# Owners and the square root placed earlier on ScalarE, keep from the minimum itself, one copy of the turned keys

## The chip, the cores and the metric

One Trainium2 chip, one core of it. The metric is the device time of one launch in microseconds (us). A NeuronCore has five engines with instruction streams of their own: PE (TensorE, matmuls and transposes), VectorE (DVE), ScalarE (ACT), GpSimd (POOL) and SyncE (SP), which in this kernel only issues transfers. They meet in semaphores.

## The reference

```python
N, HEADS, HEAD_DIM = 4096, 8, 32            # x: (4096, 256) f32, adj: (4096, 4096) int32 of 0 and 1
Q, K, V = (x @ W.T).reshape(n, HEADS, HEAD_DIM).transpose(1, 0, 2)   # for WQ, WK, WV
energy = Q @ we.T + be
attn = jnp.einsum('hqd,hkd->hqk', Q, K) * SCALING + energy
attn = softmax(attn + jnp.where(adj > 0, 0.0, -jnp.inf), axis=-1)
hard = (attn == jnp.max(attn, axis=-1, keepdims=True)).astype(jnp.float32) / HEADS
out = jnp.einsum('hqk,hkd->hqd', hard, V).transpose(1, 0, 2).reshape(n, EMBED)
return layernorm(x + out)                    # eps 1e-5
```

Each query takes, per head, the value of its one best neighbour. The adjacency is sparse and uneven: low-numbered nodes have many neighbours, later ones few.

## The kernel before, in words

A prologue (about 185 us) computes Q, keys and values for all nodes; keys (scaled by a negative factor, so that the best is a minimum) and values, split into three bf16 parts, go to a table in DRAM. The main loop then walks over *items*. A tile is 128 queries, a group is 32 queries of it (GQ), and an item is one group with up to 372 (3 x 124) of the nodes that any of its queries has as neighbour. There are 200 items. A turn of the loop holds four items, b = 0..3 (RING), and all engines run the same turns with their own code. For an item m the steps are:

- ScalarE `owners` (L624): from the edges of the group's lists, which list slot belongs to which node (`reached`, bf16); PE `planes_of` (L1207) multiplies it with the tile's words (`pay`) into `ps_x`.
- VectorE `pick` (L928 to L943): from the planes the node numbers and adjacency words (`hit`, `hit_vals`, `picks`, `bits`).
- GpSimd `gather` (L532): three indirect transfers fetch keys and values of the picked nodes into `kv`; `queries` (L525) copies the group's queries.
- ScalarE `masks` (L656) spreads the adjacency bits to bf16.
- PE `keys_across` (L1245) transposes the keys into `ps_both`, ScalarE `keys` (L662) copies them to `k_t`, PE `scores` (L1222, L1227) multiplies with the queries and adds the mask, into the same banks of `ps_both` (two buffers, one for even and one for odd items, each of two banks, one for each half of the heads).
- VectorE `tops` (L951 to L958): `best`, the minimum of each row and half; `minus_top`, the running minimum over the items of a group (`cap_of` cuts it off at a group's first item), and `keep`, 1 where the running one stays.
- ScalarE `hards` (L667): the marks, the sign of minimum minus score; PE `hards_across` (L1237) turns them into `ps_h`, ScalarE `hard_rows` (L652) copies them to `hard_t`, PE `values` (L1257) multiplies them with the values into `ps_o`.
- VectorE `merge` (L968): `o_all = o_all * keep + ps_o`.

These are staggered. In its body b of a turn PE runs planes of item b+4, scores of b+1, values of b-1, marks of b and key transposes of b+2, in that order. ScalarE runs masks of b+2, the marks' copy of b, owners of b+5, keys of b+2 (two halves, each with its own semaphore), then `hards` of b+1. VectorE runs pick of b+4, tops of b+1, merge of b-1. PE's values of an item wait for the merge of the item before (one `ps_o`).

Three other kinds of work are put between, each under a branch with a flag that SyncE plans. The *front end* turns a tile of adjacency (128 x 4096 int32) into words: ScalarE casts four quarters (`cast`, L605, `joined`), quarter 0 behind `hards` of b = 0, quarters 1 and 2 around `hards` of b = 1, quarter 3 in b = 2; PE multiplies each (L1162, `words`) one body later. The *finish* (L871 to L908 on VectorE, L1167 to L1187 on PE, L610 on ScalarE) makes the words' ranks and lists. The *rows* of a finished tile: VectorE transposes `o_all` to `o_t` in b = 1 (L974), PE turns it (`rows_back`, L1267), VectorE in b = 2 adds x and takes mean and variance (L981 to L988), ScalarE takes the square root (`row_std`, L673), and VectorE takes its reciprocal and scales the row (`norm_rows`, L992 and L995), which SyncE stores. In b = 2 ScalarE's quarter 3 stands ahead of the square root, and VectorE's `norm_rows` ahead of the merge.

## Time and profile before

| | us |
|---|---|
| three runs | 1316.35 median, 1309.31 to 1316.83 |
| the profiled execution | 1317.37, of which its span is 1315.6 |
| busy in the span: PE, weight loads | 951.6 (72%), 616.6 |
| VectorE, ScalarE, GpSimd | 929.0 (71%), 892.0 (68%), 632.8 |
| first and last start of the marks' copy (L652, 200 of them) | 185.1 and 1279.1 |
| HBM | 221 GB/s over the span |

The profile is one execution as the hardware profiler took it. Its parts: busy time per engine, the span in slices, the chain of work that ended last, the costliest groups of instructions; and the trace behind it can be asked for windows (busy time in stretches), waits (who waited for whom) and the timeline. In a timeline row the two numbers are start and duration, then engine, line, operation, out<-in with shapes, and in brackets the idle time of the engine ahead of it and what ended that. Consecutive instructions of one kind are merged (x2). "Issue" is idle time in which the engine waited for nothing that the profile shows: its own register and branch work. Granted clock is the share of full speed that TensorE was given.

### The profile page before, as it was taken

The page shows a single profiled execution, that of the slowest core. Times are in us where ns is not written, and L with a number is a line of the kernel's source. Part 1 is how long each engine was busy: PE and PEld are TensorE (multiplying, and loading weights), DVE is VectorE, ACT ScalarE, POOL GpSimd, SP SyncE. Part 2 cuts the span into 40 slices and gives each one's busy share as a digit, 9 for nine tenths or more (in the row PEclk, how much of TensorE's full clock was granted, in tenths as well). Part 3 has the DMA queues.
Part 4 walks back from the last instruction along what each step waited for, and adds up shares of the span by engine and source line. Part 5 has one row for each costly group of instructions (what it writes and reads, how often), then busy time and mean ns, then how long its engine had stood idle before and what let it go on. Part 6 is the DMA issues. An engine that isn't in the chain of part 4 may idle for free.

```text
span 1315.6 us, 51593 instructions
## 1 busy us (share of the span) xinstructions
PE 951.6 (72%) x14758; PEld 616.6 (47%) x14759; DVE 929.0 (71%) x2616; ACT 892.0 (68%) x1688; POOL 632.8 (48%) x820
## 2 busy tenths in 40 slices
PE   4787648777777778777787777777777777777771
PEld 2343325454544555455454545455445545455540
DVE  5444536777878777777787777777777777778880
ACT  1523347778777787777877877877777777766770
POOL 0000065675656566555565555554554455445650
PEclk9988877999999998989999899989998989989995
DMA  4634468677687787678777878778878787756770
GB/s 155 214 128 160 145 201 279 196 231 255 197 263 217 243 253 234 215 242 266 248 207 231 268 226 262 252 230 272 257 235 258 248 251 254 254 180 194 212 213 4
DMA packets 89522, 291.06 MB, mean 221 GB/s; under 512 B 16984, under 2 KB 30040, under 8 KB 89496
## 3 DMA queue, kind: packets, MB, share of 16 engines
q0 software_dynamic: 48720, 199.60, 49.5%
q1 hardware_dynamic: 40776, 91.15, 20.4%
q8 instruction: 12, 0.20, 0.1%
q14 instruction: 14, 0.11, 0.0%
HBM read 275.98 MB, written 14.71 MB: 221 GB/s over the span
## 4 chain that ended last, share of the span: by engine, by line
DVE 26%; PE 25%; issue 20%; ACT 15%; DVEq 7%; DMA 3%; ACTq 2%; SPq 1%; POOL 1%; POOLq 0%
DVE best L951 6%; ACT joined L605 5%; PE ps_both L1222 4%; ACT k_t L662 4%; PE ps_both L1154 4%; DVE picks L941 3%; PE ps_h L1237 3%; PE ps_o L1257 3%; DVE hit_vals L934 3%; PE ps_r L1267 3%; DVE hit L928 2%; PE ps_both L1227 2%; ACT hard L667 2%; PE ps_both L1144 2%; DVE o_all L968 2%
## 5 line engine op out<-in xcount | busy, mean ns | idle before, releaser
L532 POOL DMA_INDIRECT kv<-kv_table,picks x309 | 294.9, 954 | 231.3 <-DVE picks L941 127.6
L532 POOL DMA_INDIRECT early<-kv_table,picks x300 | 286.2, 954 | 246.0 <-DVE picks L941 131.6
L652 ACT ACTIVATE hard_t<-ps_h 128x768 bf16<-128x768 bf16 x200 | 162.0, 810 | 233.1 <-PE ps_h L1237 227.4
L667 ACT ACTIVATE hard<-ps_both,minus_top 128x384 bf16<-128x384 f32 x402 | 214.1, 594 | 32.9 <-DVE minus_top L955 30.3
L1222 PE MATMUL ps_both<-k_t,q_now 32*32 32x384 f32 x3216 | 192.6, 534 | 32.1 <-ACT k_t L662 29.0
L951 DVE TENSOR_REDUCE best<-ps_both 128x2 f32<-128x768 f32 x201 | 190.7, 949 | 28.0 <-PE ps_both L1227 17.8
L1207 PE MATMUL ps_x<-pay,reached 128*128 x1224 | 120.2, 233 | 99.6 <-ACT reached L624 93.3
L662 ACT COPY k_t<-ps_both 128x384 f32<-128x384 f32 x404 | 171.6, 479 | 14.4 <-PE ps_both L1245 14.3
L968 DVE SCALAR_TENSOR_TENSOR o_all<-o_all,keep,ps_o 128x96 f32 x400 | 107.7, 311 | 61.8 <-issue 26.5
L1207 PEld LDWEIGHTS ps_x<-pay,reached 128*128 128x128 bf16 x1224 | 83.7, 102 | 137.5 <-ACT reached L624 128.0
L605 ACT ACTIVATE joined<-adj_in,minus_half 128x1024 bf16<-128x1024 int32 x128 | 147.9, 1164 | 0.0
L1227 PEld LDWEIGHTS ps_both<-mask_of,masked 128*128 128x128 bf16 x1206 | 72.9, 102 | 140.9 <-issue 140.9
L525 POOL COPY q_now<-q_t 128x64 f32 x202 | 50.4, 249 | 167.4 <-issue 164.3
L656 ACT ACTIVATE masked<-bits,one 124x384 bf16<-124x384 uint32 x202 | 127.6, 631 | 1.4 <-issue 1.4
L624 ACT ACTIVATE reached<-iota_h,edge_of 128x384 bf16<-128x384 f16 x205 | 124.1, 605 | 1.3 <-DVE pay L906 0.8
L1227 PE MATMUL ps_both<-mask_of,masked 128*128 128x128 bf16 x1206 | 109.4, 231 | 0.0
L1237 PE MATMUL ps_h<-ident_b,hard 128*128 128x128 bf16 x1200 | 107.6, 229 | 0.0
L941 DVE TENSOR_REDUCE picks<-hit_vals 128x9 uint32<-128x288 f32 x204 | 92.7, 455 | 15.1 <-DVE hit_vals L934 9.8
L934 DVE TENSOR_TENSOR hit_vals<-ps_x,hit 128x288 f32<-128x288 f32 x204 | 93.3, 458 | 7.0
L1245 PE MATMUL ps_both<-ident_f,kv 128*128 128x128 f32 x612 | 87.6, 281 | 12.0 <-DMA kv<-kv_table,picks 12.0
L1245 PE MATMUL ps_both<-ident_f,early 128*128 128x128 f32 x600 | 90.5, 291 | 1.6 <-DMA early<-kv_table,picks 1.6
L928 DVE SCALAR_TENSOR_TENSOR hit<-ps_x,slot_of,slot 128x96 f32<-128x96 f32 x204 | 64.0, 314 | 31.5 <-issue 16.1
(145 smaller groups left out, 1309.5 us busy)
## 6 DMA issues: line engine op xcount, KB each, us to landing
adj_in<-in_adj SPq DMA_DIRECT2D x128, 512.0 KB, 5.7
kv_table<-early SPq DMA_DIRECT2D x32, 320.0 KB, 2.4
kv<-kv_table,picks POOLq DMA_INDIRECT x309
early<-kv_table,picks POOLq DMA_INDIRECT x300
early<-in_x SPq DMA_DIRECT2D x8, 512.0 KB, 6.8
x_row<-in_x SPq DMA_DIRECT2D x32, 128.0 KB
out<-y_out SPq DMA_DIRECT2D x32, 128.0 KB
plan<-places_of SPq DMA_DIRECT2D x212, 0.0 KB
```

Of the source, the lines that this page charges most:

```text
L532: pool.indirect_dma_start(kv[m % KVS][:, c, :], None, kv_table, bass.IndirectOffsetOnAxis(ap=picks[m % RING][:, c, 2:3], axis=0)).then_inc ...
L605: act.activation(joined[:, i * QW:(i + 1) * QW], adj_in[:, i * QW:(i + 1) * QW], ACT.Sign, bias=minus_half[:]).then_inc(act_cast, 1)
L652: act.activation(hard_t[m % 2][:], hard_rows_t, ACT.Copy, bias=1.0).then_inc(act_hard_t, 1)
L662: act.copy(k_t[m % 2][:, h, :], ps_s[m % 2][h][:, 0:SLOTS]).then_inc(act_kt[h], 1)
L667: done = act.activation(hard[m % 2][:, h, :], ps_s[m % 2][h][:, 0:SLOTS], ACT.Sign, bias=minus_top[m % 2][:, h:h + 1], scale=-1.0)
L951: dve.tensor_reduce(best[:], ps_both[m % 2][:, :, 0:SLOTS], AX.X, ALU.min).then_inc(dve_best, 1)
L968: done = dve.scalar_tensor_tensor(out=o_run, in0=o_run, scalar=keep[m % RING][:, h:h + 1], in1=ps_o[:, h * width:(h + 1) * width], op0=ALU ...
L1207: mm = pe.matmul(ps_x[:, c * P:(c + 1) * P], reached[m % 2][:, c * P:(c + 1) * P], pay[:].rearrange("p g i v -> p (g i v)") [:, bass.ds(va ...
L1222: pe.matmul(ps_s[m % 2][h][to:to + GQ, 0:SLOTS], q_now[m % RING][head:head + HD, h, :], k_t[m % 2][head:head + HD, h, :], start=True, stop ...
L1227: mm = pe.matmul(bank[:, c * P:(c + 1) * P], masked[m % RING][:, c, :, :].rearrange("p h q -> p (h q)"), mask_of[:], start=False, stop=(c ...
L1237: mm = pe.transpose(hard_rows_t[:, at:at + P], hard[m % 2][:, h, c * P:(c + 1) * P], ident_b[:])
L1245: mm = pe.transpose(ps_s[m % 2][h][:, c * P:(c + 1) * P], kv[m % KVS][:, c, h * P:(h + 1) * P], ident_f[:])
```

## The change

- ScalarE: in each body owners come first, ahead of masks and the marks' copy, instead of behind them.
- ScalarE: one key copy of 128 x 768 (both halves, both banks) instead of two of 128 x 384; one semaphore pair instead of two, so PE signals only when both halves are transposed.
- VectorE: `keep` compares the capped old minimum with `best` (`is_le`) instead of with the new `minus_top` (`is_equal`), and comes ahead of `minus_top`, which then has no wait of its own.
- Body b = 2: on ScalarE the square root stands ahead of the cast of quarter 3; on VectorE the merge stands ahead of `norm_rows`.

```diff
--- before.py
+++ after.py
@@ -234,8 +234,7 @@
             item_sem("dve_bits", 2), item_sem("act_masked", 1))
         landed = [sem(f"landed{i}") for i in range(KVS)]
         q_made = item_sem("q_made", 1)
-        pe_kt = [item_sem(f"pe_kt{h}", 2) for h in range(HALVES)]
-        act_kt = [item_sem(f"act_kt{h}", 1) for h in range(HALVES)]
+        pe_kt, act_kt = item_sem("pe_kt", 2), item_sem("act_kt", 1)
         pe_score = [item_sem(f"pe_score{h}", 1) for h in range(HALVES)]
         dve_best = item_sem("dve_best", 1)
         dve_minus, dve_keep = item_sem("dve_minus", 1), item_sem("dve_keep", 0)
@@ -581,7 +580,7 @@
 
         @block.scalar
         def _(act):
-            for s in act_kt + [act_reached, act_masked, act_hard, act_hard_t]:
+            for s in [act_kt, act_reached, act_masked, act_hard, act_hard_t]:
                 act.sem_inc(s, credit(s))
             act.wait_ge(dve_c, 1)
             act.activation(std[:], eps[:], ACT.Sqrt)
@@ -657,9 +656,9 @@
                                .unsqueeze(2).to_broadcast([USED, CHUNKS, HEADS4, GQ]), ACT.Relu, bias=one[0:USED],
                                scale=-1.0).then_inc(act_masked, 1)
 
-            def keys(m, due, h):
-                act.wait_ge(pe_kt[h], due(pe_kt[h]))
-                act.copy(k_t[m % 2][:, h, :], ps_s[m % 2][h][:, 0:SLOTS]).then_inc(act_kt[h], 1)
+            def keys(m, due):
+                act.wait_ge(pe_kt, due(pe_kt))
+                act.copy(k_t[m % 2][:], ps_both[m % 2][:, :, 0:SLOTS]).then_inc(act_kt, 1)
 
             def hards(m, due):
                 act.wait_ge(dve_minus, due(dve_minus))
@@ -675,8 +674,7 @@
             act.wait_ge(dve_k, 12)
             for m in range(2):
                 masks(m, for_item(m))
-                for h in range(HALVES):
-                    keys(m, for_item(m), h)
+                keys(m, for_item(m))
             hards(0, for_item(0))
 
             def turn():
@@ -685,20 +683,19 @@
                         cast(tile_of(act, r, "fe") * 16 + 16, tile_of(act, r, "fe") * QUARTERS, i)
 
                 for b in range(RING):
+                    owners(b + 5, for_loop(act, r, 5), f"ahead{b + 5}")
                     masks(b + 2, for_loop(act, r, 2))
                     hard_rows(b, for_loop(act, r, 0))
-                    owners(b + 5, for_loop(act, r, 5), f"ahead{b + 5}")
-                    for h in range(HALVES):
-                        keys(b + 2, for_loop(act, r, 2), h)
+                    keys(b + 2, for_loop(act, r, 2))
                     if b == 0:
                         with front_end_finish(act, r):
                             flags_back(tile_of(act, r, "fin") + 1)
                     if b == 1:
                         cast_quarter(1)
                     if b == 2:
-                        cast_quarter(3)
                         with rows_due(act, r):
                             row_std(tile_of(act, r, "te_done"))
+                        cast_quarter(3)
                     if b == 3:
                         take_plan()
                     hards(b + 1, for_loop(act, r, 1))
@@ -952,12 +949,11 @@
                 if between is not None:
                     between()
                 capped = cap_of[:].rearrange("p g i -> p (g i)")[:, bass.ds(at, 1)]
+                dve.scalar_tensor_tensor(out=keep[m % RING][:], in0=minus_top[(m + 1) % 2][:], scalar=capped,
+                                         in1=best[:], op0=ALU.max, op1=ALU.is_le
+                                         )._wait_ge(dve_best, due(dve_best)).then_inc(dve_keep, 1)
                 dve.scalar_tensor_tensor(out=minus_top[m % 2][:], in0=minus_top[(m + 1) % 2][:], scalar=capped,
-                                         in1=best[:], op0=ALU.max, op1=ALU.min
-                                         )._wait_ge(dve_best, due(dve_best)).then_inc(dve_minus, 1)
-                dve.scalar_tensor_tensor(out=keep[m % RING][:], in0=minus_top[(m + 1) % 2][:], scalar=capped,
-                                         in1=minus_top[m % 2][:], op0=ALU.max, op1=ALU.is_equal
-                                         )._wait_ge(dve_minus, due(dve_minus)).then_inc(dve_keep, 1)
+                                         in1=best[:], op0=ALU.max, op1=ALU.min).then_inc(dve_minus, 1)
 
             def merge(m, due, group):
                 width = PARTS * HD
@@ -1096,12 +1092,12 @@
                             words(tile_of(dve, r, "fe") * QUARTERS, tile_of(dve, r, "fe") * FIN)
                         dve.reg_add(r["fe"], r["fe"], r["fe_on"])
                         dve.reg_mov(r["fe_on"], r["fe_next"])
+                    if b > 0 or begun:
+                        merge(b - 1, for_loop(dve, r, -1),
+                              dve.snap(r[f"running{b - 1}" if b else "running_last"], min_val=0, max_val=(2 * GPT - 1) * HALVES * PARTS * HD))
                     if b == 2:
                         with rows_due(dve, r):
                             norm_rows(tile_of(dve, r, "te_done"))
-                    if b > 0 or begun:
-                        merge(b - 1, for_loop(dve, r, -1),
-                              dve.snap(r[f"running{b - 1}" if b else "running_last"], min_val=0, max_val=(2 * GPT - 1) * HALVES * PARTS * HD))
                     dve.reg_add(r["n"], r["n"], 1)
 
             turn(False)
@@ -1115,7 +1111,7 @@
 
         @block.tensor
         def _(pe):
-            for s in [pe_planes, pe_hard_t, pe_pv] + pe_kt + pe_score:
+            for s in [pe_planes, pe_hard_t, pe_pv, pe_kt] + pe_score:
                 pe.sem_inc(s, credit(s))
             pe.sem_inc(pe_words, QUARTERS)
             pe.wait_ge(dve_k, 4)
@@ -1215,7 +1211,7 @@
             def scores(m, due):
                 pe.wait_ge(dve_k, 12)
                 pe.wait_ge(q_made, due(q_made))
-                pe.wait_ge(act_kt[1], due(act_kt[1]))
+                pe.wait_ge(act_kt, due(act_kt))
                 for j in range(HEADS4):
                     for h in range(HALVES):
                         to, head = (j + h) % HEADS4 * HD, j * HD
@@ -1244,7 +1240,7 @@
                     for c in range(CHUNKS):
                         mm = pe.transpose(ps_s[m % 2][h][:, c * P:(c + 1) * P],
                                           kv[m % KVS][:, c, h * P:(h + 1) * P], ident_f[:])
-                    mm.then_inc(pe_kt[h], 1)
+                mm.then_inc(pe_kt, 1)
 
             def values(m, due):
                 pe.wait_ge(act_hard_t, due(act_hard_t))
```

## Rows read from the trace of the kernel before

**Rows 1.** Windows of three stages: stretch, length, busy us per engine, clock, DMA share, GB/s.

```profile
251.57:304.02 52.45, 40.14 (x770) 25.83 (x769) 41.72 (x110) 42.18 (x84) 37.99 (x50) 1.00 0.75 229
304.02:857.20 553.18, 420.25 (x7316) 277.75 (x7315) 421.78 (x1173) 426.45 (x806) 323.19 (x416) 0.95 0.76 240
857.20:1184.01 326.81, 240.44 (x3993) 165.41 (x3992) 251.04 (x716) 242.26 (x442) 161.66 (x208) 0.92 0.77 244
```

**Rows 2.** Waits: who for whom, us, times, longest; 300 to 1200, then stages.

```profile
ACT hard_t L652 <- PE ps_h L1237: 188.4, 156, 3.0
...
DVE rstd L992 <- ACT std L673: 34.9, 13, 3.2
...
DVE pay L906 <- PE ps_x L1207: 14.1, 13, 2.0
DVE rstd L992 <- ACT std L673: 7.6, 12, 0.9
```

**Rows 3.** Timeline of one light item, ScalarE and PE's scores.

```profile
346.72 0.81 ACT L652 ACTIVATE hard_t<-ps_h 128x768 bf16<-128x768 bf16 x1 [0.85 <-PE ps_h L1237]
...
347.42 0.60 ACT L624 ACTIVATE reached<-iota_h,edge_of 128x384 bf16<-128x384 f16 x1
...
347.93 0.85 ACT L662 COPY k_t<-ps_both 128x384 f32<-128x384 f32 x2
...
348.92 0.88 PE L1222 MATMUL ps_both<-k_t,q_now 32*32 32x384 f32 x16 [0.28 <-ACT k_t L662]
...
351.09 0.81 ACT L652 ACTIVATE hard_t<-ps_h 128x768 bf16<-128x768 bf16 x1 [0.85 <-PE ps_h L1237]
```

**Rows 4.** Timeline of VectorE: small steps, and the ends of a light turn.

```profile
332.59 0.15 DVE L883 COPY ends<-ps_x 128x4 f32<-128x4 f32 x1
...
332.66 0.15 DVE L884 SCALAR_TENSOR_TENSOR count_f<-ps_x,flag 128x4 f32<-128x4 f32 x1
...
341.29 0.31 DVE L928 SCALAR_TENSOR_TENSOR hit<-ps_x,slot_of,slot 128x96 f32<-128x96 f32 x1
...
348.24 0.22 DVE L955 SCALAR_TENSOR_TENSOR minus_top<-minus_top,cap_of,best 128x2 f32<-128x2 f32 x1
...
348.50 0.22 DVE L958 SCALAR_TENSOR_TENSOR keep<-minus_top,cap_of 128x2 f32<-128x2 f32 x1
...
357.61 0.31 DVE L928 SCALAR_TENSOR_TENSOR hit<-ps_x,slot_of,slot 128x96 f32<-128x96 f32 x1
```

**Rows 5.** Timeline of GpSimd: first gathers of two items, four apart.

```profile
400.02 0.97 POOL L532 DMA_INDIRECT early<-kv_table,picks  x1 [3.10 <-DVE picks L941]
...
416.31 0.97 POOL L532 DMA_INDIRECT kv<-kv_table,picks  x1 [0.29 <-issue]
```

**Rows 6.** Timeline of b = 2 in a turn with cast and rows.

```profile
649.29 0.18 DVE L988 BATCH_NORM_AGGREGATE mean_var<-stats 128x2 f32<-128x6 f32 x1
...
650.71 0.22 DVE L958 SCALAR_TENSOR_TENSOR keep<-minus_top,cap_of 128x2 f32<-128x2 f32 x1
...
652.17 1.17 ACT L605 ACTIVATE joined<-adj_in,minus_half 128x1024 bf16<-128x1024 int32 x1
...
653.22 0.30 ACT L673 ACTIVATE std<-mean_var,eps 128x1 f32<-128x1 f32 x1
...
653.62 0.16 DVE L992 RECIPROCAL rstd<-std 128x1 f32<-128x1 f32 x1 [2.69 <-ACT std L673]
```

**Rows 7.** PE's turned rows in two full turns, an item's ends, one window.

```profile
962.05 0.81 ACT L652 ACTIVATE hard_t<-ps_h 128x768 bf16<-128x768 bf16 x1 [0.76 <-PE ps_h L1237]
...
964.96 2.53 PE L1267 MATMUL ps_r<-ident,o_t 128*128 128x128 f32 x12 [2.28 <-DVE o_t L974]
...
971.16 0.81 ACT L652 ACTIVATE hard_t<-ps_h 128x768 bf16<-128x768 bf16 x1 [2.51 <-PE ps_h L1237]
...
1041.65 1.60 PE L1267 MATMUL ps_r<-ident,o_t 128*128 128x128 f32 x12 [0.70 <-DVE o_t L974]
...
964.96:967.50 2.54, 2.54 (x14) 2.54 (x15) 1.80 (x5) 1.63 (x4) 1.04 (x2) 0.59 0.96 325
```

## The prediction, made before the change was run

> **What bounds the kernel now.** I read the windows by stage first, because the share of busy time is an average over stages with different limits. The main loop runs from 185 to 1285 us: 200 items of work, 50 turns of four items b = 0..3. [rows 1] cuts it where the kind of turn changes. The 3 turns from 251.57 carry no front-end work ("light"): 52.45 / 3 = 17.48 us a turn, 4.37 an item. The 26 turns from 304.02 mostly alternate between a turn with casts and output rows and one with the finish of a tile's lists: 553.18 / 26 = 21.3. The 13 turns from 857.20 carry everything ("full"): 326.81 / 13 = 25.1. The reader is to see that no engine is full anywhere: in the light stretch ScalarE has the largest share of the three that compute, 42.18 / 52.45 = 0.80, and VectorE and PE stand beside it. So what counts is the loop between engines, and the next view is the waits [rows 2]. ScalarE waits 188.4 us in 156 of some 160 items for PE's turned marks (ps_h). VectorE waits for hardly anything but the standard deviation: 34.9 us in 13 turns of the alternating stage, 7.6 in the full one, where it also waits 14.1 for the planes. Everything else in front of VectorE is its own issue and semaphore time, so in both stages VectorE is nearly always the engine that is late.
>
> The light item in order of time [rows 3] shows the other loop. Marks are turned, ScalarE copies them (346.72), makes owners (347.42), copies keys (347.93 for both halves), and only then may the scores start (348.92); PE ends its item with the next turned marks, and the next copy starts at 351.09. That is 4.37 us, closed on itself: owners lie on it although the planes they feed are needed by nobody soon.
>
> **Owners first.** Nothing is removed. Owners start 0.51 us before the key copy does (347.42 to 347.93), so the loop loses 0.51 of its 4.37. They go in front of ScalarE's wait for the marks, which is 188.4 / 156 = 1.2 us an item and about 0.85 in a light one; that wait is the cover. With the cover gone they cost their 0.51 again. Masks stay ahead of the key copy in ScalarE's order, so PE's one wait for the key copy still stands for both. Planes start earlier and no longer wait for owners.
>
> **One key copy.** Two copies span 0.85 [rows 3]. No 128x768 f32 copy stands in the trace; bounds: the 768-wide bf16 copy on the same engine takes 0.81 (351.09), and the pair with an overlap like that of small steps (0.08, [rows 4]) undone would be 0.93. I take 0.81, the row it is nearest to in width and engine: -0.04 an item, at worst +0.08. Both halves of the key transposes must now be done before it starts; PE runs them right behind the marks, while ScalarE copies these for 0.70 us (346.72 to 347.42), so I add nothing; without that cover it would cost the second half of them. By the Trainium skill, "ScalarE: Activation LUTs", What ACT_TABLE_LOAD costs, an activation costs a fixed part and 0.833 ns an element, and neighbours overlap by 93 ns: it would make the pair 0.92 and the single copy 0.83. The row has 0.85 for the pair, and the measurement decides.
>
> The PE and ScalarE loop becomes 4.37 - 0.51 - 0.04 = 3.82 an item, 15.3 a light turn.
>
> **Keep from the minimum.** Before, minus_top starts, keep starts 0.26 later because it waits for it [rows 4]. Now keep goes first and minus_top has no wait. The trace has small instructions without a wait: the second of two of 0.15 us starts 0.07 after the first [rows 4], 0.08 less than the duration. So minus_top should start 0.22 - 0.08 = 0.14 after keep. VectorE saves 0.26 - 0.14 = 0.12 an item where register and branch work follows, as it does in three of four items (the branches around the tile work stand ahead of the merge there), and up to 0.26 where the merge follows at once: (3 x 0.12 + 0.26) / 4 = 0.155 an item. Below nothing: if minus_top cannot overlap, it starts 0.22 later and the gain is 0.04. The price is that minus_top ends 0.14 (at most 0.26) later for ScalarE's marks; in the light item ScalarE is busy with keys then, so it is hidden, and where VectorE is late it eats into the same 0.12.
>
> A light turn of VectorE alone takes 16.32 [rows 4], so it becomes 15.7. GpSimd's issue of gathers is a third loop: with its list always ready, a turn from one first gather to the same one four items on takes 16.29 [rows 5]. So **a light turn goes to 16.3, not 15.3**: gain 1.2, and GpSimd holds it.
>
> **Square root ahead of the cast, merge ahead of the row's end.** In a cast turn [rows 6] VectorE has its mean at 649.5, finishes keep at 650.93 and then stands until 653.62, since ScalarE runs a 1.17 us cast (652.17) before the square root (653.22). The merge is behind that, and PE's words and values behind the merge. Moved, the square root starts right behind the key copy: at 653.22 - 1.05, less 0.51 and 0.04 for the steps above, 651.6. VectorE fills 0.54 of the rest with the merge (650.93 + 0.3 to 651.8) and then has its input at 651.9. The wait of 34.9 / 13 = 2.7 falls to some 0.7 at most, a gain of 2.0, and the merge itself comes 2.7 or more earlier. The cast now ends 0.2 later relative to the key copy, and the marks of the item behind both as before. In full turns VectorE is late, so ScalarE may now stand at the square root until the mean is there, with the cast and marks behind it; but those marks need minus_top, which VectorE makes 1.3 us after the mean, and square root and cast take 0.2 + 1.05. Cost: nothing, gain the 7.6 us of waits.
>
> **The sum**, by stage:
> - 185 to 252, 3 turns with casts but no rows. Nearly every item runs on the PE and ScalarE loop; 12 x 0.55 = 6.6, less a third because VectorE is close behind: -4.5.
> - 252 to 304, 3 light turns: -3.6.
> - 304 to 857, 26 turns (104 items): VectorE is busy or issuing for 553.2 - 34.9; keep gives 104 x 0.155 = 16, the square root 34.9 - 13 x 0.7 = 26. PE's own path in the stage is 553 less 104 x 0.55 and 13 x 1 for the item behind the square root, about 483, under VectorE's 511; I take 3 off for items in which PE is nevertheless last: -39.
> - 857 to 1184, 13 full turns: VectorE's 14.1 us of waits for planes start at PE's output rows, which wait for VectorE's o_t, so keep's gain of that item is only waited away: 3 x 0.12 a turn is 4.7, the square root 7.6: -12.
> - 1184 to 1285, 5 turns, VectorE nearly full: 20 x 0.155 = -3.
>
> Together -62. The profiled execution took 1317.4, 1.0 above the median of the runs: 1316.35 - 62 = 1254.
>
> **Rivals.**
> *The VectorE edit gives nothing* (0.20). If minus_top behind keep costs as much as keep did behind minus_top, 16, 4.7 and 3 us go, and the marks come 0.26 later: 1254 + 24 = 1278. Against it is the 0.07 of [rows 4]; for it, that those two are of another form. The Trainium skill, "VectorE: DVE Perf Modes", The DRAIN you can't avoid, says the semaphore between chained VectorE operations costs nothing; by that rule this rival is the outcome. The rows speak against it.
> *The gathers hold more than the light turns* (0.08). GpSimd needs 16.3 a turn against a new mean of (553 - 39) / 26 = 19.8, so only bunched lists hurt: it stood 3.10 us for one list and then had four in a row ready [rows 5]. If half of that wait comes back at PE in each of the 12 pairs of turns, 1254 + 18 = 1272.
> *VectorE gains the full 0.26 and PE follows* (0.12): 0.1 x 160 items more, and no residual wait (9): 1229.
> *Nothing measurable* (0.05): the loop refills its slack with VectorE's lateness everywhere, the gain is only the first two stages, 1308.
> *Slower* (0.05): PE's clock. PE comes earlier to its wait for o_t, while VectorE doesn't. In one turn PE idled 2.28 there and then turned the rows in 2.53 us at a granted clock of 0.59, near the 1.2 GHz level; in another it idled 0.70 and took 1.60 [rows 7]. That item ran 9.11 us in all (962.05 to 971.16), against 25.1 / 4 = 6.3 on average in its stage, 2.8 more. It decides from 62 / 2.8 = 22 turns more in that state; with the 25 or so turns with output rows that are not in it yet, +70 against -62: 1324.
>
> **Chances and range.** The forecast's case holds 0.50, with its own range of 1243 to 1268. To leave out no more than 0.2 the range takes in the first two rivals and most of the third: 1236 to 1283. What a measurement of this kernel tells from no change is about 1%, 13 us: faster 0.88, within 0.06, slower 0.06.
>
> **What would show it.** Right: a light item under 4.2 and at or above 4.05, with GpSimd never waiting for PE in the light stretch; ScalarE's wait for the marks under 0.7 us an item; planes that wait for owners gone; the key copy at 0.80 to 0.83; minus_top starting 0.14 behind keep; VectorE's wait for the standard deviation under 15 us in all; full turns near 24.2. Wrong: a copy of 0.95 or more; minus_top 0.22 or more behind keep; ScalarE waiting for minus_top in most items; many more row turns at half clock.

## The result, and the profile after

| | before | changed |
|---|---|---|
| median of 4 runs, us | 1316.3 (1309.3 to 1316.8) | 1246.9 (1243.8 to 1250.2) |
| profiled execution's span, us | 1315.6 | 1246.6 |
| granted clock, whole span | 0.92 | 0.94 |

The ratio is 0.9485, with a 95% interval of 0.9443 to 0.9526: 69 us off, where 62 were predicted (1254, with a range of 1236 to 1283). The first view is again the windows by stage. The columns are those of [rows 1]: stretch, length, busy us per engine (PE, weight load, VectorE, ScalarE, GpSimd), clock, DMA share, GB/s.

```profile
245.55:293.30 47.75, 39.01 (x768) 25.94 (x768) 40.26 (x111) 42.20 (x72) 37.69 (x49) 1.00 0.81 249
293.30:808.02 514.72, 405.59 (x7316) 271.60 (x7317) 414.65 (x1173) 421.46 (x702) 324.59 (x418) 0.98 0.80 258
808.02:1119.55 311.53, 232.60 (x3993) 162.18 (x3992) 246.11 (x716) 241.81 (x390) 162.46 (x208) 0.95 0.80 256
```

ScalarE's busy time is within 1.2% of that in each stage of [rows 1] (42.18, 426.45 and 242.26 us there), and VectorE's fell by 1.5, 7 and 5 us. The stages got shorter by 4.7, 38.5 and 15.3. So what went is for the most part idle time between engines, as the prediction read it. PE's busy time fell by 1.1, 14.7 and 7.8 us with the same number of matmuls. The granted clock was 0.98 instead of 0.95 in the second stage and 0.95 instead of 0.92 in the third, so part of what went there can be PE's clock; how much was not separated. By its own terms, each stage cut where the first copy of marks of its first turn starts:

| stage | before | after | measured | predicted |
|---|---|---|---|---|
| up to the loop | 185.14 | 185.56 | +0.4 | 0 |
| 3 turns with casts, no rows | 66.43 | 59.99 | -6.4 | -4.5 |
| 3 light turns | 52.45 | 47.75 | -4.7 | -3.6 |
| 26 mixed turns | 553.18 | 514.72 | -38.5 | -39 |
| 13 full turns | 326.81 | 311.53 | -15.3 | -12 |
| the rest | 131.59 | 127.05 | -4.5 | -3 |
| sum | | | -69.0 | -62 |

The waits, as in [rows 2] (who waited for whom, us, times, longest); first 300 to 1100, the same stretch of the loop as 300 to 1200 before, less two turns:

```profile
ACT hard_t L651 <- PE ps_h L1233: 69.4, 93, 3.5
ACT hard L666 <- DVE minus_top L955: 66.6, 65, 2.2
...
DVE pay L903 <- PE ps_x L1203: 19.1, 13, 2.7
...
DVE hit L925 <- PE ps_x L1203: 17.1, 21, 2.0
...
DVE rstd L988 <- ACT std L672: 4.2, 10, 0.5
```

and the full stage alone, 808.02 to 1119.55:

```profile
PE ps_r L1263 <- DVE o_t L970: 31.6, 13, 2.6
...
DVE pay L903 <- PE ps_x L1203: 19.5, 13, 2.7
```

The first of these in the full stage of the kernel before (857.20 to 1184.01):

```profile
PE ps_r L1267 <- DVE o_t L974: 20.7, 13, 2.3
```

ScalarE's wait for the marks fell from 188.4 us to 69.4. Beside it, it now waits for VectorE's minus_top, 66.6 us in 65 of the 152 items of this stretch (23.9 us in 30 before): PE's and VectorE's paths decide about equally when ScalarE goes on. VectorE's wait for the standard deviation fell from 42.5 in two stages to 4.2 (4.6 over the whole run). What grew, in the full turns, is PE's wait for the turned rows o_t, 20.7 to 31.6, and VectorE's for the planes behind them, 14.1 to 19.5. In the other turns VectorE's pick now waits for the planes too: 17.1 us in the stretch above, 4.9 in that of the kernel before.

The light item in order of time, the one of [rows 3] after the change:

```profile
285.68 0.81 ACT L651 ACTIVATE hard_t<-ps_h 128x768 bf16<-128x768 bf16 x1 [0.35 <-PE ps_h L1233]
...
286.18 0.22 DVE L952 SCALAR_TENSOR_TENSOR keep<-minus_top,cap_of,best 128x2 f32<-128x2 f32 x1
286.32 0.22 DVE L955 SCALAR_TENSOR_TENSOR minus_top<-minus_top,cap_of,best 128x2 f32<-128x2 f32 x1
286.39 0.79 ACT L661 COPY k_t<-ps_both 128x768 f32<-128x768 f32 x1
286.51 0.54 DVE L964 SCALAR_TENSOR_TENSOR o_all<-o_all,keep,ps_o 128x96 f32 x2
...
287.33 0.88 PE L1218 MATMUL ps_both<-k_t,q_now 32*32 32x384 f32 x16 [0.69 <-ACT k_t L661]
...
288.01 0.63 ACT L623 ACTIVATE reached<-iota_h,edge_of 128x384 bf16<-128x384 f16 x1
288.51 0.63 ACT L655 ACTIVATE masked<-bits,one 124x384 bf16<-124x384 uint32 x1
289.49 0.81 ACT L651 ACTIVATE hard_t<-ps_h 128x768 bf16<-128x768 bf16 x1 [0.35 <-PE ps_h L1233]
```

The loop from marks to marks is 289.49 - 285.68 = 3.81 us; 3.82 was worked out from [rows 3]. Owners (288.01) now sit where ScalarE used to wait, and the wait left for the marks is 0.35 instead of 0.85: 0.5 of it was the cover. This item is of the quickest kind. The 12 light items take 47.75 / 12 = 3.98 on average.

### The profile page after: what moved, and what is told of

The parts are those of the page before. It is cut to its first block, busy times and chain, and to the rows that moved or that the text cites. A ratio compares the mean times of both kernels' runs of the same rounds, so it can differ in the third digit from the quotient of the medians.

```text
span 1246.6 us, 51239 instructions
## 1 busy us (share of the span) xinstructions
PE 924.1 (74%) x14758; PEld 604.8 (49%) x14759; DVE 912.7 (73%) x2616; ACT 885.3 (71%) x1486; POOL 634.1 (51%) x820
## 4 chain that ended last, share of the span: by engine, by line
DVE 35%; PE 19%; issue 18%; DMA 8%; DVEq 7%; ACT 7%; POOL 3%; ACTq 1%; POOLq 1%; SPq 1%
DVE best L948 8%; DVE picks L938 5%; DVE hit_vals L931 4%; PE ps_r L1263 4%; PE ps_both L1150 4%; DVE hit L925 3%; ACT joined L604 3%; DMA kv<-kv_table,picks 3%; DMA early<-kv_table,picks 3%; PE ps_both L1140 2%; PE ps_both L1241 2%; DVE o_all L964 2%; PE ps_x L1203 2%; DMA be_sb<-in_L_gnn_be 2%; PE ps_both L1218 1%
## 5 line engine op out<-in xcount | busy, mean ns | idle before, releaser
L1218 PE MATMUL ps_both<-k_t,q_now 32*32 32x384 f32 x3216 | 183.1, 510 | 54.6 <-ACT k_t L661 53.1
L661 ACT COPY k_t<-ps_both 128x768 f32<-128x768 f32 x202 | 161.2, 798 | 30.6 <-PE ps_both L1241 29.9
L1203 PE MATMUL ps_x<-pay,reached 128*128 x1224 | 115.6, 226 | 39.7 <-issue 32.3
L1223 PEld LDWEIGHTS ps_both<-mask_of,masked 128*128 128x128 bf16 x1206 | 70.0, 99 | 132.0 <-issue 132.0
L623 ACT ACTIVATE reached<-iota_h,edge_of 128x384 bf16<-128x384 f16 x205 | 127.0, 619 | 2.9 <-issue 1.6
L655 ACT ACTIVATE masked<-bits,one 124x384 bf16<-124x384 uint32 x202 | 124.5, 616 | 0.0
L1233 PE MATMUL ps_h<-ident_b,hard 128*128 128x128 bf16 x1200 | 103.0, 223 | 7.2 <-ACT hard L666 5.3
L1223 PE MATMUL ps_both<-mask_of,masked 128*128 128x128 bf16 x1206 | 105.2, 225 | 0.0
L938 DVE TENSOR_REDUCE picks<-hit_vals 128x9 uint32<-128x288 f32 x204 | 92.7, 454 | 13.8 <-DVE hit_vals L931 8.4
L925 DVE SCALAR_TENSOR_TENSOR hit<-ps_x,slot_of,slot 128x96 f32<-128x96 f32 x204 | 64.1, 314 | 39.9 <-PE ps_x L1203 23.9
L1263 PE MATMUL ps_r<-ident,o_t 128*128 128x128 f32 x384 | 59.5, 314 | 43.9 <-DVE o_t L970 43.9
```

What stands on the lines that cost most here:

```text
L661: act.copy(k_t[m % 2][:], ps_both[m % 2][:, :, 0:SLOTS]).then_inc(act_kt, 1)
L938: dve.tensor_reduce(picks[m % RING][:], hit_vals[:], AX.X, ALU.add).then_inc(dve_picks, 1)
L1203: mm = pe.matmul(ps_x[:, c * P:(c + 1) * P], reached[m % 2][:, c * P:(c + 1) * P], pay[:].rearrange("p g i v -> p (g i v)") [:, bass.ds(va ...
L1218: pe.matmul(ps_s[m % 2][h][to:to + GQ, 0:SLOTS], q_now[m % RING][head:head + HD, h, :], k_t[m % 2][head:head + HD, h, :], start=True, stop ...
L1223: mm = pe.matmul(bank[:, c * P:(c + 1) * P], masked[m % RING][:, c, :, :].rearrange("p h q -> p (h q)"), mask_of[:], start=False, stop=(c ...
```

## The experiments

Ratios are against the kernel before on the same chip. Differences are from the changed kernel's 1246.9; that holds across chips, since the kernel before took 1317.3 to 1317.4 on those of the later runs and 1316.3 on that of the changed kernel. With intervals of some 0.35% on each ratio, under about 7 us can't be told between two of these kernels.

**A chip apart.** The first four runs, each part of the change alone on the kernel before, fell on a chip on which the kernel before itself took 1808.6 us (1781 to 1835) at a granted clock of 0.77. They decide nothing on a kernel that takes 1316 us, and the questions were asked again on other chips.

Owners alone:

```diff
                 for b in range(RING):
+                    owners(b + 5, for_loop(act, r, 5), f"ahead{b + 5}")
                     masks(b + 2, for_loop(act, r, 2))
                     hard_rows(b, for_loop(act, r, 0))
-                    owners(b + 5, for_loop(act, r, 5), f"ahead{b + 5}")
```

> The kernel before with only the owners moved to the front of ScalarE's body. Theory of three loops (the PE and ScalarE loop of 4.37 us an item, VectorE's own 4.08, GpSimd's 4.07; VectorE late in nearly all heavy turns): light items go to VectorE's 4.1; in the alternating turns the PE and ScalarE path gets 0.5 an item shorter, VectorE's own work does not, and what is gained is a shorter wait for the standard deviation (2.7 us a turn before, about 1 after): in all 30 to 40 us off 1316. Rival, every item is bound by the PE and ScalarE loop: 200 x 0.51 = 102 us off. Rival, the owners' move pays in light and cast turns without rows alone: about 10 us off.

Measured: 1725.7 us, ratio 0.966 (0.949 to 0.983). PE's values in that trace, in order of time:

```profile
916.23 0.20 PE L1257 MATMUL ps_o<-early,hard_t 124*32 124x96 bf16 x1 [0.55 <-issue]
916.98 0.20 PE L1257 MATMUL ps_o<-early,hard_t 124*32 124x96 bf16 x1 [0.55 <-issue]
918.77 0.24 PE L1257 MATMUL ps_o<-early,hard_t 124*32 124x96 bf16 x1 [1.58 <-issue]
```

On the other chips the 24 matmuls of this group run in 0.44 us. Here single ones stand 0.55 to 1.58 us behind nothing that the trace shows. Why stays open.

The key copy alone (all that the change's diff does to `keys`, `pe_kt` and `act_kt`). Measured: 1819.5, ratio 1.015 (1.002 to 1.029):

> The kernel before with only the one key copy (128x768) for both halves. Theory: 0.05 us an item (copy of 0.80 against a pair of 0.85) on the items that the PE and ScalarE loop holds, about half of them: 3 to 8 us off. Rival, the coupling of both halves costs more than it gives since the owners still stand in front of it: no change, or up to 5 us slower.

Keep alone (the diff under "Keep back", reversed, on the kernel before). Measured: 1912.6 (1880 to 1921), with no ratio; the same kernel ran again on another chip as "Keep only", below:

> The kernel before with only keep taken from the minimum and put ahead of minus_top. Theory: VectorE's work gets 0.13 to 0.26 us an item shorter, but in the alternating turns VectorE then only waits longer for the standard deviation, and light items stay at 4.37: it pays in the 13 full turns and the five behind them alone, 5 to 10 us off. Rival, VectorE binds everywhere outside the light turns: 170 x 0.155 = 26 us off.

The two moves of b = 2 alone (the diff under "Rows back", reversed, on the kernel before). Measured: 1899.7, ratio 1.059 (1.042 to 1.077), against the expectation. Taken back from the changed kernel on another chip the same moves cost 18 us, so the loss here may well be this chip's; as they weren't run alone on another, that isn't shown:

> The kernel before with only the b = 2 orders changed: square root ahead of the cast on ScalarE, merge ahead of the row's end on VectorE. Theory: the wait for the standard deviation (42.5 us in all) goes nearly away and PE's words come about 1 us earlier in each of 30 turns: 25 to 35 us off. Rival, hidden: the item behind it stays at 6.0 us because casts and marks on ScalarE are the path: under 10 us off. If the four parts simply add up, the four gains sum to the 69 us of the change; if the loops cover one another, they sum to more or less than that.

**Owners back** behind the masks, in the changed kernel (the diff above reversed):

> The changed kernel with the owners alone moved back behind the marks' copy. Theory of three loops: the PE and ScalarE loop goes back from 3.81 to 4.32 us an item, the light turns back to about 17.3 us, the cast turns to 0.5 more in each of b = 0 and b = 1, full turns hardly change since VectorE holds them: 25 to 35 us slower than the changed kernel's 1247, so 1272 to 1282. Rival, every item pays the 0.51: +100, 1345. Rival, VectorE holds everything but the light and first turns: +10, 1257.

Measured: 1268.4 (1265.4 to 1271.0), ratio 0.963 (0.960 to 0.966): 21.5 us slower than the changed kernel, 4 under the theory's range and far from both rivals. So the edit is worth that in company of the others. The wait that was said to go is back (300 to 1100):

```profile
ACT hard_t L651 <- PE ps_h L1233: 138.7, 126, 3.1
...
PE ps_x L1203 <- ACT reached L623: 60.8, 87, 1.3
...
DVE rstd L988 <- ACT std L672: 19.0, 12, 2.1
```

Its stages are 65.4, 51.7, 530.6 and 310.3: all of the loss is in the first three, and the full turns don't mind. The light turns take 17.24 us on average against 47.75 / 3 = 15.9: the loop of PE and ScalarE holds them again. The last row says what the 15.9 us in the mixed stage go along with. VectorE's wait for the standard deviation is back at 19.0 us, where the changed kernel has 4.2, although the square root is still ahead of the cast: owners behind the marks' copy also delay the square root. So these two parts of the change share one wait. The granted clock of the mixed stage was 0.93 here and 0.98 in the changed kernel; what of the 15.9 is due to that was not separated. In the light stage it was 1.00 in both.

**Keep back** behind minus_top:

```diff
-  dve.scalar_tensor_tensor(out=keep, in0=minus_top[(m + 1) % 2], ..., in1=best, op1=ALU.is_le)
-     ._wait_ge(dve_best, ...)
   dve.scalar_tensor_tensor(out=minus_top[m % 2], in0=minus_top[(m + 1) % 2], ..., in1=best, op1=ALU.min)
+     ._wait_ge(dve_best, ...)
+  dve.scalar_tensor_tensor(out=keep, in0=minus_top[(m + 1) % 2], ..., in1=minus_top[m % 2],
+                           op1=ALU.is_equal)._wait_ge(dve_minus, ...)
```

> The changed kernel with minus_top first and keep from it, behind its wait, as before. Theory: VectorE's own work is 0.13 to 0.26 us an item longer, and VectorE holds the alternating, the full and the last turns: 16 + 4.7 + 3 by the prediction's terms, 15 to 25 us slower than 1247, so 1262 to 1272; light turns stay at 16.1. Rival, minus_top comes 0.13 earlier for ScalarE's marks, which wait for it 86 us in all now, and that outweighs VectorE's time: within 4 us of 1247.

Measured: 1283.9 (1281.6 to 1286.4), ratio 0.975 (0.971 to 0.978): 37 us slower, beyond what the theory allowed. A merge of this kernel, in order of time on VectorE, with PE's values behind it:

```profile
265.88 0.22 DVE L952 SCALAR_TENSOR_TENSOR minus_top<-minus_top,cap_of,best 128x2 f32<-128x2 f32 x1
...
266.14 0.22 DVE L955 SCALAR_TENSOR_TENSOR keep<-minus_top,cap_of 128x2 f32<-128x2 f32 x1
...
266.76 0.54 DVE L965 SCALAR_TENSOR_TENSOR o_all<-o_all,keep,ps_o 128x96 f32 x2 [0.40 <-DVE keep L955]
...
267.35 0.44 PE L1254 MATMUL ps_o<-kv,hard_t 124*32 124x96 bf16 x24 [0.29 <-DVE o_all L965]
```

and one of the same kind in the changed kernel:

```profile
262.09 0.22 DVE L952 SCALAR_TENSOR_TENSOR keep<-minus_top,cap_of,best 128x2 f32<-128x2 f32 x1
262.23 0.21 DVE L955 SCALAR_TENSOR_TENSOR minus_top<-minus_top,cap_of,best 128x2 f32<-128x2 f32 x1
262.71 0.54 DVE L964 SCALAR_TENSOR_TENSOR o_all<-o_all,keep,ps_o 128x96 f32 x2 [0.27 <-issue]
```

From the first small step to the merge: 0.88 against 0.62. The same interval over all merges that follow the small steps directly is 0.71 on average with keep back (143 merges) and 0.45 in the changed kernel (143); it comes in classes, by how much register and branch work stands between, and each class moved by the same amount: 0.59 to 0.33, 0.88 to 0.62, 0.98 to 0.72. So 0.26 us an item goes, with and without that work. The reading: the engine's register work for the merge starts once keep has been let go; a keep that waits for minus_top holds it up for 0.26, one that waits for nothing lets it run while both small steps execute.

The run undoes two things at once, the wait and the order of the two. Keep first without a wait was run, minus_top first without one was not, so that it is the wait and not the order is read from the intervals, not shown by a run.

By stage keep back costs 2.5, 1.1, 13.8 and 12.6, and 5.8 at the end (62.5, 48.8, 528.5, 324.2 and 132.8). The 12.6 in 13 full turns is 0.97 a turn. By item (means here and below are over 14 full turns, since one of them lies in the mixed stage): b = 0, 2 and 3 take 5.36, 5.09 and 6.05 instead of 5.05, 4.81 and 5.47, and b = 1 takes 8.49 instead of 8.70. So b = 1 gained nothing by the edit, as predicted, and the other three gained 1.17 together, not 3 x 0.12. The granted clock of the full stage was 0.91 here against 0.95; whether some of the 1.17 is due to it was not separated.

**Keep only**: the diff above reversed, on the kernel before, on another chip than the first four runs:

> The kernel before with only keep from the minimum, ahead of minus_top (the same kernel as keep_alone). Taking this part out of the changed kernel cost 37 us. VectorE saves 0.26 us an item by the traces. Theory, the loops cover one another: in the kernel before light turns are held by PE and ScalarE at 4.37 and the alternating turns by the wait for the standard deviation, so alone it pays only where VectorE waits for nobody, the 14 full turns (1.0 each) and part of the rest: 12 to 25 us off 1317, 1292 to 1305. Rival, the part is worth the same alone as in company: 37 off, 1280. The prediction's term for it, read for this kernel, is 8 to 24 off.

Measured: 1299.2 (1289.9 to 1301.7), ratio 0.985 (0.979 to 0.990): 18 off. Alone the edit is worth half of what it is worth last. Its stages show it: 66.1 and 52.5 in the first two, unchanged, most likely since owners on ScalarE's path hold them (ScalarE waited for PE's marks 156.9 us in 129 items between 300 and 1100); -4.9 and -9.0 in the next two.

**Rows back**: the cast ahead of the square root, and the merge behind the row's end, in the changed kernel:

```diff
                     if b == 2:
+                        cast_quarter(3)
                         with rows_due(act, r):
                             row_std(tile_of(act, r, "te_done"))
-                        cast_quarter(3)
...
-                    if b > 0 or begun:
-                        merge(...)
                     if b == 2:
                         with rows_due(dve, r):
                             norm_rows(tile_of(dve, r, "te_done"))
+                    if b > 0 or begun:
+                        merge(...)
```

> The changed kernel with both orders of b = 2 as before: cast ahead of the square root on ScalarE, row's end ahead of the merge on VectorE. Theory: the wait for the standard deviation comes back in the 12 turns with casts and rows (about 2 us each, 26 in all by the prediction's term) and in part in the 14 full ones (7.6): 20 to 34 us slower than 1247, 1267 to 1281; light turns and turns with the finish alone stay. Rival, with owners first ScalarE is early enough, and the wait is hidden: under 8 us slower.

Measured: 1265.3 (1261.5 to 1267.1), ratio 0.960 (0.956 to 0.963): 18.5 slower, 2 under the theory's range and far over the rival's. VectorE's wait is back (300 to 1100), where the changed kernel has 4.2:

```profile
DVE rstd L988 <- ACT std L672: 24.3, 13, 2.3
```

14 of the 18.5 lie in the mixed stage (528.7 against 514.7), where the prediction's sum has 26, and 1.3 in the full one (312.9 against 311.5), where it has 7.6. In the full stage this wait is 0.3 us in all even with the old order: with owners first ScalarE is early enough there, as the rival had it.

**Key back**: two copies of turned keys again, in the changed kernel (the `keys` part reversed):

> The changed kernel with two key copies of 128x384 and two semaphore pairs again. Theory: the pair spans 0.85 where the one copy takes 0.80, and the first half may start when three of the six key transposes are done; the 0.05 an item counts where the PE and ScalarE loop holds, about half the items: 2 to 8 us slower than 1247. Rival, in the changed kernel ScalarE waits 15 to 30 us in all for both halves of the key transposes, and a first half that starts earlier wins that back: up to 10 us faster than 1247.

Measured: 1248.6 (1245.4 to 1250.1), ratio 0.947 (0.944 to 0.951): nothing that can be measured. The copies themselves (durations min, median, max in ns) in the changed kernel and in this one:

```profile
L661 ACT COPY k_t<-ps_both x202: 786/794/820, 174.2 to 1210.9; 128x768 f32<-128x768 f32 x101
```

```profile
L662 ACT COPY k_t<-ps_both x404: 466/484/531, 174.6 to 1211.9; 128x384 f32<-128x384 f32 x135
```

**Wide queries**: is GpSimd's gather loop close to holding the kernel? Its copy of the queries writes four times the width; the extra copies are read by nobody, nothing is left out.

```diff
-        q_now = [sb(f"q_now{i}", [P, HALVES, GQ], F32) for i in range(RING)]
+        q_now = [sb(f"q_now{i}", [P, 4, HALVES, GQ], F32) for i in range(RING)]
...
-                pool.tensor_copy(q_now[m % RING][:], q_t[:, :, bass.ds(at, GQ)]).then_inc(q_made, 1)
+                pool.tensor_copy(q_now[m % RING][:], q_t[:, :, bass.ds(at, GQ)].unsqueeze(1).to_broadcast(...)).then_inc(q_made, 1)
```

> The changed kernel with GpSimd's copy of the queries written four times as wide (256 instead of 64 elements, the rest unused): only GpSimd's own work in an item grows, by some 0.3 to 0.6 us (the 64-wide one takes 0.25). Theory, GpSimd's issue of gathers holds the light turns alone (16.1 us, PE waits for a landing there): light turns grow by 4 times the copy's growth to 17.3 to 18.5, alternating turns by less than 1, full ones not: 8 to 20 us slower in all. Rival, gathers hold the alternating turns too: 104 + 20 items by the full growth, 40 to 75 us slower. Rival, they hold nothing: no change.

The copy went from a median of 242 to 402 ns:

```profile
L524 POOL COPY q_now<-q_t x202: 393/402/499, 162.5 to 1209.6; 128x256 f32 x101
```

Measured: 1254.3 (1252.4 to 1263.8), ratio 0.955 (0.950 to 0.959): 7 slower, at the edge of what can be told, of the 200 x 0.16 = 32 that a GpSimd on the path everywhere would cost. The probe came out smaller than meant (0.16 instead of 0.3 to 0.6), so it only bounds: if all the loss were the gathers', they would hold a quarter of the items by the medians (7 / 32), and half by the slowest run (17 us). The stages speak for less. They are 61.1, 48.4, 510.8 and 318.9: the light stage, which the theory was about, lost 0.6 of at most 12 x 0.16 = 1.9, the mixed one nothing, and the full one 7.4, where the theory has none. In that stage PE's turned rows took over 2.1 us (1.60 is usual) in 7 of the 13 turns, against 4 in the changed kernel, and the granted clock was 0.93 against 0.95. So the 7 us can as well be PE's clock, and no loss by the gathers is shown beyond the light turns.

**Turned rows first.** In full turns of the changed kernel item b = 1 takes 8.70 us on average and the other three 5.05, 4.81 and 5.47 (before: 7.57, and 5.92, 6.08, 5.55). In it, in order of time:

```profile
862.82 0.35 DVE L893 TENSOR_SCALAR n_items<-rounded 128x4 f32 x1
...
863.85 0.98 DVE L970 STREAM_TRANSPOSE o_t<-o_all 128x768 f32<-128x768 f32 x1 [0.68 <-DVE n_items L893]
...
864.88 1.70 PE L1263 MATMUL ps_r<-ident,o_t 128*128 128x128 f32 x12 [2.59 <-DVE o_t L970]
...
866.13 1.05 ACT L666 ACTIVATE hard<-ps_both,minus_top 128x384 bf16<-128x384 f32 x2 [1.91 <-DVE minus_top L955]
...
868.07 0.29 DVE L903 CAST pay<-ps_x 128x128 f32 x1 [1.47 <-PE ps_x L1203]
...
871.07 0.81 ACT L651 ACTIVATE hard_t<-ps_h 128x768 bf16<-128x768 bf16 x1 [1.85 <-PE ps_h L1233]
```

PE stands 2.59 for o_t, because VectorE first makes the ranks and lists of a tile that PE asks for later; then VectorE stands 1.47 for PE, and ScalarE 1.85. The edit:

```diff
                     if b == 1:
-                        with front_end_finish(dve, r):
-                            ranks(fin() + 1, fin() * FIN, None)
-                            lists(fin() * FIN, table(), fin() * GPT)
                         with rows_due(dve, r):
...
                                 turn_rows(GPT, for_loop(dve, r, -2)(dve_merge))
+                        with front_end_finish(dve, r):
+                            ranks(fin() + 1, fin() * FIN, None)
+                            lists(fin() * FIN, table(), fin() * GPT)
```

> The changed kernel with VectorE's turn of o_all to o_t (1 us) ahead of the ranks and lists in b = 1 instead of behind them. In the 13 full turns of the changed kernel b = 1 takes 7.2 to 10.7 us, since PE stands 2 us and more for o_t, then turns the rows (1.5 to 2.5), and only then makes the planes that VectorE waits for. Theory, that chain from VectorE through PE back to VectorE holds the full turns: PE's rows now run beside VectorE's ranks and lists, b = 1 loses 1.5 to 2 us in each of 14 turns: 15 to 28 us faster than the changed kernel, 1219 to 1232. Rival, VectorE's own work holds the full turns and the order within it is no matter: within 3 us of 1247.

Measured: 1218.3 (1215.4 to 1221.0), ratio to the kernel before 0.927 (0.923 to 0.930), 28.5 us under the changed kernel: the best of all. The same place:

```profile
937.57 0.98 DVE L970 STREAM_TRANSPOSE o_t<-o_all 128x768 f32<-128x768 f32 x1 [0.29 <-issue]
...
938.60 1.60 PE L1263 MATMUL ps_r<-ident,o_t 128*128 128x128 f32 x12 [0.57 <-DVE o_t L970]
...
941.26 1.05 ACT L666 ACTIVATE hard<-ps_both,minus_top 128x384 bf16<-128x384 f32 x2 [1.31 <-DVE minus_top L955]
...
942.06 0.29 DVE L903 CAST pay<-ps_x 128x128 f32 x1 [0.30 <-issue]
...
944.61 0.81 ACT L651 ACTIVATE hard_t<-ps_h 128x768 bf16<-128x768 bf16 x1 [0.25 <-PE ps_h L1233]
```

and the full stage, waits and window (columns as above):

```profile
PE ps_r L1263 <- DVE o_t L970: 3.2, 7, 0.6
```

```profile
798.93:1088.99 290.06, 225.26 (x3993) 153.59 (x3992) 244.92 (x717) 240.24 (x391) 162.86 (x209) 0.99 0.84 276
```

31.6 us of PE's waits became 3.2, item b = 1 takes 7.02, the full stage 290.1 instead of 311.5, and the mixed one 506.5 instead of 514.7. The granted clock in the full stage is 0.99 instead of 0.95. In the changed kernel PE's turned rows took 2.93 us, near twice the usual 1.60, in 4 of its 13 turns, each behind a wait of 2.2 to 2.6 (nine others behind waits of 2.0 to 2.6 took 1.60 to 1.70):

```profile
839.65 2.93 PE L1263 MATMUL ps_r<-ident,o_t 128*128 128x128 f32 x12 [2.54 <-DVE o_t L970]
```

Here, where the longest wait is 0.6, they took 1.60 in all 13. The turns with those slow rows got 2.0 to 2.9 us shorter, the others 1.1 to 1.7. So both the order and the clock are in the 21.5 us of this stage.

**Turned rows ahead of the pick too**: the same block moved one step further, ahead of `pick(b + 4, ...)`:

> VectorE's turn of o_all to o_t moved further, ahead of the pick in b = 1. Against turn_first (1218) PE has o_t another 1.6 us earlier. Theory, in turn_first PE no longer waits for o_t, so nothing more is gained, and the pick, and with it the gather of its item, comes 0.9 us later: within 5 us of 1218. Rival, PE is still held by o_t in the turns with rows: another 5 to 12 us off, 1206 to 1213.

Measured: 1226.7 (1222.0 to 1227.6), ratio 0.931 (0.928 to 0.934): 8 slower than the run above, so neither within 5 of it nor the rival. It loses in full turns (295.3, b = 1 at 7.58). The pick feeds the gathers, and it was moved behind 1 us of transpose; that this is the way it loses was not looked into further. The granted clock of the full stage was 0.95 again, not 0.99.

## Why the prediction was right, point by point

- **Which engine is late.** Right in the main. No engine is full, most of what went is idle time between them, and the runs that undo owners or the moves of b = 2 bring back the wait that was named for each.
- **The sum.** 69 against 62 is closer than its terms are. It gives owners, with the key copy, 8 us directly (the first two stages) and a share in the square root's term, keep 24 and the moves of b = 2 34; undone last they cost 21.5, 37 and 18.5. The mixed stage, 38.5 against 39, is in part luck. VectorE's small steps gave 104 x 0.26 = 27 where 16 stood, and its wait for the standard deviation fell by 34.9 - 4.2 = 31 where 26 stood, together 58. For items in which PE or ScalarE is last 3 was taken off, and it had to be 19; 13 of these are VectorE's new wait for the planes (4.1 to 17.1 in this stage). In the full stage 4.7 for keep and 7.6 for the square root stood for what the undoing runs put at 12.6 and 1.3.
- **Owners first.** Right in mechanism, and the quickest light items have the loop at 3.81 against 3.82. The planes' waits for owners are gone, and 60.8 us of them come back with the order undone. Its worth in the mixed stage runs through the square root (19.0 us of that wait come back as well), which the prediction has in its start of the square root ("less 0.51"), not under owners.
- **One key copy.** Right in size: 0.794 us where 0.81 was taken between 0.81 and 0.93. The 0.04 to 0.05 an item is too little to be seen in the time. By the formula of the Trainium skill, "ScalarE: Activation LUTs", What ACT_TABLE_LOAD costs, it would be 0.826 as an estimate; the measured 0.794 is 4% under it.
- **Keep from the minimum.** Right in sign, mis-sized. minus_top starts 0.13 to 0.14 behind keep, as 0.14 was worked out from [rows 4]. The term that failed is "0.12 an item where register and branch work follows": it took that work as fixed behind the last small step, so that only the steps themselves could save. It starts earlier by the whole 0.26, and VectorE saves 0.26 in every item instead of 0.155 on average. In the full stage that is 12.6 us by keep back where 4.7 stood in the sum, and it is the likeliest reason that the stage beat its -12. Over 200 items it is 21 us more of VectorE's path, and the residual below is 9 more, but only 7 of the 30 came: this is the third rival's mechanism, with 1229, and the time did not go that far. ScalarE and PE hold part of the items (ScalarE waits for minus_top in 65 of 152 only, and VectorE now waits for planes), which would do it; that it accounts for all the 23 was not shown.
- The Trainium skill, "VectorE: DVE Perf Modes", The DRAIN you can't avoid, says that the semaphore costs nothing extra, measured there on eight copies. The rival that this rule stood beside (1278) did not come: with the wait the second step starts 0.26 behind the first, without it 0.14, and the edit is worth 18 us alone and 37 in company, its order included. The same section also says that an operation that is not held starts before the one in front has drained, and the 0.14, less than the 0.22 that the first step takes, agrees with that.
- **A light turn is held by GpSimd at 16.3.** Half right. The three light turns took 16.20, 16.31 and 15.24. The last is the bare PE and ScalarE loop, 4 x 3.81; back-to-back first gathers of items in the first of them stand 3.88 apart (246.68, 250.56, 254.44), 15.5 a turn, so the 16.29 of [rows 5] was no floor. Neither was VectorE's 15.7: it saved 0.26 an item, not 0.155, and 16.32 - 4 x 0.26 = 15.3. GpSimd's list is nearly always ready there: it waited 0.6 us in 2 instances for each of its two kinds of buffer. Its issue is near enough to the loop that either can be the one, and wide queries showed no item beyond the light turns that it holds.
- **Square root ahead of the cast.** Right for the wait: 34.9 and 7.6 us of waits became 4.2, where at most 15 were allowed, and in a full turn the reciprocal starts at 873.51 right behind the merge (872.96, 0.54). Of the residual, 13 x 0.7 = 9 us, 4.2 were there. For the time the term was too large: 34 stood in the sum, and the old order costs 18.5, since owners first take away part of the same wait (24.3 us of it come back, not 42.5).
- **Full turns.** 311.53 / 13 = 23.96 against "near 24.2", though by another sum (above): luck in part. That keep's gain in b = 1 is only waited away was right: VectorE's wait for the planes grew from 14.1 to 19.5 in the stage, and PE's wait for o_t from 20.7 to 31.6. What was not said is that this was the next bound, and that a change of order on VectorE, not a saving, would lift it.
- **Rivals.** The clock: item b = 1 did lengthen, 7.57 to 8.70, as the slower rival had it, but the clock of the full stage rose from 0.92 to 0.95 and the other three items shrank by 2.2 together. Turned rows of over 2.1 us came in 5 of the 13 full turns before and in 4 after. Its price of 2.8 a turn was set against the mean of all four items; against the other b = 1 items of its own stage (9.0 on average with slow rows, 6.7 without) it is 2.3, longer waits for o_t included. Gathers: no mixed turn lost by the probe. Of the signs of being wrong, none came up; ScalarE waits for minus_top in 65 items of 152, not in most. Of the signs of being right two missed: light items are 3.98 on average, under the 4.05, and ScalarE's wait for the marks is 69.4 / 93 = 0.75 where it waits, counted as the 1.2 was, not under 0.7.
- **What stays open.** The undone parts cost 21.5, 37, 18.5 and 1.7, together 79 against the 69 that they give, and keep's 37 is 18 where owners still hold the loop: the loops cover one another, and how much of the second 18 is each partner's was not separated. In two mixed turns item b = 3 took 6.90 and 8.54 where 4.55 is usual. In the trace PE waits there for the rows of a gather (0.83 and 1.22 us) and for itself (0.75 and 1.36), and then its 16 score matmuls take 1.53 instead of 0.88; the granted clock in the second of them, from 502.2 to 507.6, is 0.50. The wait comes first and the low clock behind it, as with o_t.

## What to carry to other kernels

Where no engine is full, find for each stage the loop that closes on itself, and take off it what nobody on it needs soon: put back on it, the same 0.5 us an item cost nothing in full turns, and all of its 21 us in the others. When a saving only turns into a wait of the other engine, look at the order of the work behind that wait: moving two blocks past each other gave 28 us where the whole change gave 69. And a part of a change can be worth more together with the others than alone when they shorten different loops over the same items: the one part that was measured both ways gave 18 alone and 37 last. So don't read the worth of a part from one run alone, and look at the stages and the clock before a small loss is put down to what was edited.

## What the runs showed of the hardware

- A small VectorE instruction that waits for the one in front of it costs more than the 0.12 by which it starts later: the next instruction came 0.26 later, with and without register and branch work between (0.33 to 0.59, 0.62 to 0.88, 0.72 to 0.98). The order of the two changed with the wait.
- In the full turns of the changed kernel PE stood 2.0 to 2.6 us for o_t and then turned the rows in 1.60 to 1.70 us in nine turns and in 2.93 in four. With waits of 0.6 at most it was 1.60 in all 13, and the granted clock of the stage 0.99 instead of 0.95.
- One chip ran the kernel before in 1808.6 us instead of 1316 at a granted clock of 0.77 instead of 0.92, with gaps of 0.55 to 1.58 us between matmuls of one group that show as PE's own issue. The moves of b = 2, which cost 18 us elsewhere when taken back, came out there as 5.9% slower. The cause is open.
